# Split-precision Gram stage of a cross-attention kernel: one mixed product summed by whole rows, and a ring of ten high-high blocks

## The reference, cut to what matters

```
g     = g_w @ x_2 + g_b          # 256 x 1024
theta = theta_w @ x + theta_b    # 256 x 1024
phi   = phi_w @ x_2 + phi_b      # 256 x 1024
W     = theta.T @ phi / 1024     # 1024 x 1024
y     = (W @ g.T).T              # 256 x 1024
out   = batchnorm(w_w @ y + w_b) + x   # 512 x 1024, float32
```

## Time and profile before

| | us |
|---|---|
| median of 3 runs | 845.85 |
| lowest, highest | 845.2, 846.4 |
| span of the profiled execution, first to last instruction | 845.1 |
| TensorE matmul busy | 816.8 (97%) |
| TensorE weight loads busy | 708.9 (84%) |
| VectorE busy | 493.7 (58%) |
| ScalarE busy | 268.7 (32%) |
| GpSimd busy | 511.0 (60%) |

### The profile page before, as it was taken

How to read it: one execution, slowest core, us unless ns; L and a number is a source line. 1 busy time by engine, 2 the same in 40 slices (tenths; PEclk the granted TensorE clock), 3 DMA queues, 4 the chain that set the end, 5 groups by cost and what they waited for, 6 DMA issues and landing times.

```text
span 845.1 us, 12602 instructions
## 1 busy us (share of the span) xinstructions
PE 816.8 (97%) x4397; PEld 708.9 (84%) x4397; DVE 493.7 (58%) x885; ACT 268.7 (32%) x442; POOL 511.0 (60%) x351
## 2 busy tenths in 40 slices
PE   4589999999999999999999999999999999999997
PEld 2478888989889898988989888898988889898886
DVE  3865475565657556565655656565655766556254
ACT  1532333342233334223323412333242233323121
POOL 0893865668376565847666585666748556673400
PEclk9798999999999999999999999999999999999999
DMA  9825534254442434543253554325345432630202
GB/s 207 206 92 100 196 68 137 99 116 182 99 175 71 130 120 99 199 99 149 86 138 124 99 199 98 125 96 132 145 99 199 83 119 100 145 150 0 101 1 99
DMA packets 53010, 103.10 MB, mean 122 GB/s; under 512 B 2410, under 2 KB 35844, under 8 KB 52996
## 3 DMA queue, kind: packets, MB, share of 16 engines
q1 hardware_dynamic: 52996, 102.91, 41.5%
HBM read 69.35 MB, written 33.55 MB: 122 GB/s over the span
## 4 chain that ended last, share of the span: by engine, by line
PE 92%; DVE 3%; DMA 2%; POOL 1%; issue 1%; SPq 1%; ACT 0%; DVEq 0%; POOLq 0%; ACTq 0%
PE gbank L502 49%; PE wbank L502 42%; DMA ctx_sb<-in_ctx_dram 2%; PE wbank L602 1%; DVE ctxT_lo L390 1%; POOL x_lo L262 1%; DVE ctxT L354 1%; DVE gram_hi L432 1%; PE wbank L534 0%; SPq L199 0%; SPq L190 0%; POOL ctxT_lo L246 0%; POOL ctx_sum L254 0%; ACT x_hi L279 0%; DVE junk L420 0%
## 5 line engine op out<-in xcount | busy, mean ns | idle before, releaser
L246 POOL TENSOR_TENSOR ctxT_lo<-ctxT,ctxT_hi 128x512 fp32r<-128x512 f32 x120 | 158.5, 1320 | 147.8 <-ACT ctxT_hi L279 147.0
L262 POOL TENSOR_TENSOR x_lo<-x_sb,x_hi 128x1024 fp32r<-128x1024 f32 x64 | 151.8, 2406 | 110.1 <-ACT x_hi L279 110.1
L502 PE MATMUL gbank<-ctxT_hi,ctxT_lo 128*128 128x512 f32 (+3 forms) x512 | 165.8, 324 | 0.0
L502 PE MATMUL gbank<-ctxT_lo,ctxT_hi 128*128 128x512 f32 (+3 forms) x512 | 165.5, 323 | 0.0
L502 PE MATMUL gbank<-ctxT_hi 128*128 128x512 f32 (+3 forms) x512 | 163.4, 319 | 0.0
L279 ACT ACTIVATE ctxT_hi<-ctxT 128x512 fp32r<-128x512 f32 x128 | 80.3, 633 | 260.9 <-PE gbank L502 205.7
L254 POOL TENSOR_TENSOR ctx_sum<-ctx_sum,ctxT 128x512 f32<-128x512 f32 x112 | 155.7, 1390 | 0.9 <-POOL ctx_sum L249 0.2
L492 DVE SCALAR_TENSOR_TENSOR x_sb<-wbank,const,x_sb 128x512 f32<-128x512 f32 x128 | 89.4, 746 | 77.7 <-PE wbank L502 77.7
L354 DVE STREAM_TRANSPOSE ctxT<-ctx_sb 128x512 f32<-128x512 f32 x128 | 83.5, 689 | 56.7 <-POOL ctx_sum L254 28.1
L502 PEld LDWEIGHTS gbank<-ctxT_hi 128*128 128x128 f32 x512 | 97.6, 191 | 7.0 <-issue 0.2
L502 PEld LDWEIGHTS gbank<-ctxT_lo,ctxT_hi 128*128 128x128 f32 x512 | 96.8, 189 | 6.8
(11 more groups left out here) (92 smaller groups left out, 1342.7 us busy)
## 6 DMA issues: line engine op xcount, KB each, us to landing
ctx_sb<-in_ctx_dram SPq DMA_DIRECT2D x64, 512.0 KB, 8.4
x_sb<-in_x_dram SPq DMA_DIRECT2D x16, 2048.0 KB, 7.9
out_dram<-x_sb SPq DMA_DIRECT2D x64, 512.0 KB, 2.6
x_sb<-in_L_xattn_w_w_dram SPq DMA_DIRECT2D x1, 512.0 KB, 3.8
x_sb<-in_L_xattn_g_w_dram SPq DMA_DIRECT2D x1, 512.0 KB, 5.2
phi_nat<-in_L_xattn_phi_w_dram SPq DMA_DIRECT2D x1, 512.0 KB, 13.7
stage<-in_L_xattn_theta_w_dram SPq DMA_DIRECT2D x1, 512.0 KB, 12.5
bp_row<-in_L_xattn_phi_b_dram SPq DMA_DIRECT2D x1, 128.0 KB, 11.6
```

The source lines that it names most:

```text
L246: nc.gpsimd.tensor_tensor(ctxT_lo[:, c, :], src, f(ctxT_hi[:, c, :]), ALU.subtract).then_inc(ctxT_lo_made, 1)
L262: nc.gpsimd.tensor_tensor(x_lo[:, k, :], x_sb[par][:, k, :], f(x_hi[:, k, :]), ALU.subtract).then_inc(x_lo_made, 1)
L502: return nc.tensor.matmul(dst, lhsT, rhs, start=start, stop=stop, skip_group_check=True)
```

## The change

The high-high product is summed first, for all eight chunks, in four matmuls per chunk. It is held as ten of the sixteen 128 x 128 blocks, three, three and four in the three `gbank` banks, chosen as a ring: row blocks 0, 1 and 2 of widths 3, 3 and 2, and for row block 3 the blocks (3, 0) and (3, 3), read by one matmul with a step.

Then M = high x low is summed by whole rows, row block by row block, eight matmuls of 512 columns each, in two alternating `wbank` banks. ScalarE copies each row of M to the new tile `mt`. The product low x high is the transpose of M. It is no longer multiplied out: ten matmuls of `mt` against an identity (`turned`) add transposed blocks of M to `gbank`, and VectorE adds M itself when it takes the bank to `stage` (`PLAIN`, four additions). ScalarE, no longer VectorE, makes `gram_hi`. `t_hi` and `t_lo` now lie in `mt`.

`seq` and `own` are gone: each use has a fixed bank, and each wait names the event. S now has bank `wbank[4]`, is made after the rows of M, and theta(1) uses that bank next. TensorE therefore waits for `s_taken` ahead of theta(1). On VectorE the S work is split: the four reductions to `s_col` stand after `low_lo`, the two to `p1_raw` and the `p1` that raises `s_taken` stand after the last `t_lo`. The context chunks are four, two and two, at the start, after theta(0) and after `p1`, where they were six and two. `gram_chunk` is raised only in the last row of M. TensorE also waits ahead of the first batch until VectorE has freed all ten set-up groups.

```diff
+    HELD = [(0, 0), (0, 1), (0, 2), (1, 1), (1, 2), (1, 3), (2, 2), (2, 3), (3, 0), (3, 3)]
+    UPPER = len(HELD) * P
+    BANK_SPAN = [(0, 3 * P), (3 * P, 6 * P), (6 * P, UPPER)]
+    LOWER = [(3, 2), (0, 3), (1, 0), (2, 1), (3, 1), (2, 0)]
+
+
+    TURNED_EARLY = [(0, 0, 0), (1, 1, 0), (2, 2, 0), (3, 1, 1), (4, 2, 1), (6, 2, 2), (8, 0, 3)]
+    TURNED_LATE = [(5, 3, 1), (7, 3, 2), (9, 3, 3)]
+    LAST_OF_BANK = (2, 5, 9)
+
+    PLAIN = [(0, 3, 0), (3, 6, 5), (6, 9, 10), (9, 10, 15)]
     T_BANK = [0, 1, 2, 0]
     Q_BANK = [1, 2]
-    T_ORDER = [3, 2, 1, 0]
-
+    T_ORDER = [2, 3, 1, 0]
...
-        t_hi = sb("t_hi", [P, KC, CI], F32R)
-        t_lo = sb("t_lo", [P, KC, CI], F32R)
+        mt = sb("mt", [P, KC, C], F32R)
...
+        m_flat = mt[:, :, :].rearrange("p a b -> p (a b)")
+        t_hi = mt[:, 0:2, :].rearrange("p a (b c) -> p (a b) c", b=2)
+        t_lo = mt[:, 2:4, :].rearrange("p a (b c) -> p (a b) c", b=2)
...
+
+        M_BANK = [wbank[0], wbank[3], wbank[0], wbank[3]]
+        S_BANK = wbank[4]
+        LOW_BANK = [wbank[0], wbank[3]]
+        TH_BANK = [[wbank[1], wbank[2]], [wbank[4], wbank[0]]]
+        OUT_BANK = [[wbank[1], wbank[2]], [wbank[3], gbank[0]], [wbank[4], wbank[0]], [wbank[1], wbank[2]]]
...
-                if nxt:
-                    for c in range(EARLY):
-                        act.wait_ge(gram_chunk, (CH - 1) * b + (c + 1))
+                def next_hi(c):
+                    if nxt:
+                        act.wait_ge(gram_chunk, CH * b + (c + 1))
                         ctx_hi(b + 1, c)
+
+                for i in range(KC):
+                    if i < KC - 1:
+                        act.wait_ge(m_done, (KC - 1) * b + (i + 1))
+                    else:
+                        next_hi(0)
+                        act.wait_ge(gram_chunk, CH * b + CH)
+                    hi(mt[:, i, :], M_BANK[i][:, :], m_made)
+                next_hi(1)
                 for i, (a, z) in enumerate(BANK_SPAN):
-                    act.wait_ge(gram_row, 3 * b + (i + 1))
-                    hi(stage[:, a:z], gbank[i][:, 0:z - a], gram_f32)
+                    act.wait_ge(gram_f32, 3 * b + (i + 1))
+                    hi(gram_hi[:, a:z], stage[:, a:z], gram_hi_made)
+                next_hi(2)
                 for g in range(2):
-                    act.wait_ge(work_done, seq(b, G_LOW + g + 1))
+                    act.wait_ge(low_done, 2 * b + (g + 1))
                     hi(low_hi[:, 3 * g:3 * g + 3, :],
...
+                next_hi(3)
                 theta(0)
-                if nxt:
-                    for c in range(EARLY, CH):
-                        ctx_hi(b + 1, c)
+                next_hi(4)
+                next_hi(5)
                 for r, m in enumerate(T_ORDER):
                     act.wait_ge(t_taken, KC * b + (r + 1))
...
                 if nxt:
                     dve.wait_ge(in_ctx, b * (16 * QT) + 32 * QT)
-                    for c in range(EARLY):
...
-                nc.vector.tensor_tensor(p1[:, :], p1_raw[:, :], nbp_col[:, :], ALU.add).then_inc(work_free, 1)
+                for i, (a, z, m) in enumerate(PLAIN):
+                    g = min(i, 2)
+                    if i < 3:
+                        dve.wait_ge(gram_row, 3 * b + (i + 1))
+                    at = a * P - BANK_SPAN[g][0]
+                    ins = nc.vector.tensor_tensor(stage[:, a * P:z * P], gbank[g][:, at:at + (z - a) * P],
+                                                  f(m_flat[:, m * P:(m + z - a) * P]), ALU.add)
+                    if i != 2:
+                        ins.then_inc(gram_f32, 1)
                 for i, (a, z) in enumerate(BANK_SPAN):
...
+                dve.wait_ge(s_done, b + 1)
+                for i in range(KC):
+                    nc.vector.tensor_tensor_reduce(junk[:, 0, i * P:(i + 1) * P], S_BANK[:, i * P:(i + 1) * P], ident[:, :], 1.0, 0.0,
+                                                   ALU.mult, ALU.add, s_col[:, i:i + 1]).then_inc(s_made, 1)
                 theta(0)
                 if nxt:
-                    for c in range(EARLY, CH):
-                        transpose_chunk(b + 1, c, True)
+                    transpose_chunk(b + 1, 4, True)
+                    transpose_chunk(b + 1, 5, True)
+                dve.wait_ge(s_made, 6 * b + KC)
...
                     if r > 0:
                         t_lo_part(r - 1)
                 t_lo_part(KC - 1)
+                for k in range(KI):
+                    nc.vector.tensor_tensor_reduce(junk[:, k, :], S_BANK[:, :], phi_nat[:, k, :], 1.0, 0.0,
+                                                   ALU.mult, ALU.add, p1_raw[:, k:k + 1]).then_inc(s_made, 1)
+                dve.wait_ge(s_made, 6 * b + 6)
+                nc.vector.tensor_tensor(p1[:, :], p1_raw[:, :], nbp_col[:, :], ALU.add).then_inc(s_taken, 1)
+                if nxt:
+                    transpose_chunk(b + 1, 6, True)
+                    transpose_chunk(b + 1, 7, True)
 
...
                 for k in range(KI):
...
             pe.wait_ge(zb_taken, 1)
+            pe.wait_ge(work_free, SETUP_GROUPS)
+            pe.wait_ge(ident_r_made, 1)
...
+                def hi_of(c, i):
+                    return ctxT_hi[:, c, i * P:(i + 1) * P]
+
+                pe.wait_ge(work_free, NO * b + (SETUP_GROUPS + 4 - NO))
...
+                    pe.wait_ge(ctxT_hi_made, CH * b + (c + 1))
+                    mm(gbank[0][:, 0:3 * P], hi_of(c, 0), ctxT_hi[:, c, 0:3 * P], c == 0, False)
+                    mm(gbank[1][:, 0:3 * P], hi_of(c, 1), ctxT_hi[:, c, P:4 * P], c == 0, False)
+                    mm(gbank[2][:, 0:2 * P], hi_of(c, 2), ctxT_hi[:, c, 2 * P:4 * P], c == 0, False)
+                    mm(gbank[2][:, 2 * P:4 * P], hi_of(c, 3),
+                       ctxT_hi[:, c, :].rearrange("p (k q) -> p k q", q=P)[:, 0::3, :], False, False)
+
+                for i in range(KC):
+                    if i < 2:
+                        pe.wait_ge(work_free, NO * b + (SETUP_GROUPS + (6, 3)[i] - NO))
+                    else:
+                        pe.wait_ge(m_made, KC * b + (i - 1))
+                    for c in range(CH):
+                        if i == 0:
+                            pe.wait_ge(ctxT_lo_made, CH * b + (c + 1))
+                        ins = mm(M_BANK[i][:, :], hi_of(c, i), ctxT_lo[:, c, :], c == 0, c == CH - 1)
+                        if i == KC - 1:
+                            ins.then_inc(gram_chunk, 1)
+                    if i < KC - 1:
+                        ins.then_inc(m_done, 1)
+
+                pe.wait_ge(work_free, NO * b + (SETUP_GROUPS + 5 - NO))
+                pe.wait_ge(sum_split, 2 * b + 2)
+                mm(S_BANK[:, :], ones_r[:, :], sum_hi[:, :], True, False)
+                mm(S_BANK[:, :], ones_r[:, :], sum_lo[:, :], False, True).then_inc(s_done, 1)
+
+                def turned(blocks):
+                    for place, j, i in blocks:
+                        ins = mm(gram_bank(place), mt[:, j, i * P:(i + 1) * P], ident_r[:, :], False,
+                                 place in LAST_OF_BANK)
+                        if place in LAST_OF_BANK:
                             ins.then_inc(gram_row, 1)
...
+                pe.wait_ge(m_made, KC * b + 3)
+                turned(TURNED_EARLY)
+                pe.wait_ge(m_made, KC * b + 4)
+                turned(TURNED_LATE)
...
+                        if k == 0 and m == 0:
+                            pe.wait_ge(work_free, NO * b + SETUP_GROUPS)
+                        if k == 0 and m == 1:
+                            pe.wait_ge(s_taken, b + 1)
+                            pe.wait_ge(low_lo_made, 2 * b + 1)
...
                 pe.wait_ge(gram_lo_made, 3 * b + 3)
+                pe.wait_ge(low_lo_made, 2 * b + 1)
                 t_block(0)
-                pe.wait_ge(work_free, seq(b, G_LOW + 1))
                 t_block(1)
+                pe.wait_ge(low_lo_made, 2 * b + 2)
                 t_block(2)
-                pe.wait_ge(work_free, seq(b, G_LOW + 2))
                 pe.wait_ge(t_taken, KC * b + 1)
                 t_block(3)
                 theta(1, (0, 1))
...
                 pe.wait_ge(q_lo_made, KI * b + 1)
+                pe.wait_ge(th_lo_made, NT * b + NH)
+                pe.wait_ge(low_lo_made, 2 * b + 2)
+                pe.wait_ge(t_taken, KC * b + 4)
...
                 for m in (2, 3):
+                    if m == 3:
+                        pe.wait_ge(work_free, NO * b + (SETUP_GROUPS + NH))
```

More of the change, by code:

```diff
@@ L40, in xattn_kernel @@
     RING = 4
-    EARLY = 6
     assert CH * 32 == QN and NH * HALF == N
[L45 to L50, removed]
+    HELD = [(0, 0), (0, 1), (0, 2), (1, 1), (1, 2), (1, 3), (2, 2), (2, 3), (3, 0), (3, 3)]
[6 more added lines that the diff above has]
+    PLAIN = [(0, 3, 0), (3, 6, 5), (6, 9, 10), (9, 10, 15)]
     T_BANK = [0, 1, 2, 0]
     Q_BANK = [1, 2]
-    T_ORDER = [3, 2, 1, 0]
+    T_ORDER = [2, 3, 1, 0]
     NW = 5
     SETUP_GROUPS = 10
[L58 to L62, removed]
+    NO = KC * NH
```

(36 more changed lines are left out.)

70 lines of the change are left out of this document (25 added, 45 removed).

## The result

The changed kernel takes 918.5 us (median of 4 runs, 918.0 to 919.25) against 846.1 before on the same chip: a ratio of 1.085, 95% interval 1.084 to 1.0865. It is slower, by 72 us. The forecast was 926 in 884 to 948.

The account below looks back on a forecast made before the run. TensorE was taken to bound the kernel, any stall paid in full. Middle batch: -2.2 Gram, +5.4 stall, +2.4 clock = +5.6 us; 14 of them +78.4, last +2.1, first +0.3, on 845.1: span 925.9, forecast 926, range 884 to 948.

Parts of the forecast that it names:

- Gram stage: TensorE's Gram work per batch: 13.5 us in place of 15.75, a saving of 2.2, ends 0 to 2.3.
- The stepped operand: Gram matmul read with a step: might cost up to twice, 1.0 us more per batch; taken as ordinary.
- Its waits, and the split: New Gram waits and VectorE's split of G before the T blocks: no stall, split priced at zero, ends 0 to 1.5 us.
- the rival of a second stall: Ahead of the T blocks, where the split has no slack: 1.5 us more per batch, 949 us; chance 0.10.
- The wait ahead of theta(1): TensorE waits for `s_taken`, raised by VectorE's late `p1`: a 5.4 us stall per batch, ends 3.1 to 6.5.
- half of a shift of VectorE's T work: Four `s_col` reductions ahead of `th_lo` delay VectorE's T work by 0 to 0.6 us; half went into the stall.
- The clock: Behind the theta(1) stall the clock falls to half in every batch: 2.4 us each, ends 0 to 3.4.
- The sum: Whole kernel: middle batch +5.6 us, 14 of them +78.4, last +2.1, first +0.3; total +80.8, span 925.9.
- From the span to the time: Whole run: the runs' median lies 0.75 us above the span, so 925.9 becomes about 926.5, stated as 926.
- The clock holds: Behind the theta(1) stall: stall paid, no clock fall; middle batch +3.2 us, total about 890; chance 0.10.
- VectorE is not held up: T blocks without GpSimd in VectorE's way: stall 3.1 us, clock loss 1.8, total about 883 us; chance 0.10.
- Faster: `s_taken` comes less than 2.2 us after the last T block; hidden wholly, about 805 us; chance 0.04.

Follow-up runs that it names:

- the filler kernel: The changed kernel with 20 matmuls of 512 columns ahead of TensorE's wait for `s_taken`, into a bank nobody reads before it is overwritten: 886.3 us, ratio 1.047.
- the late chunks: The changed kernel with context chunks 4 and 5 moved behind `p1`, together with 6 and 7, so GpSimd rests beside the T blocks: 880.2 us, ratio 1.040.
- the other bank: The changed kernel with theta(1) in `wbank[3]` in place of S's `wbank[4]`, the outputs swapping the two, no engine's order changed: 810.7 us, ratio 0.958.

## Why the prediction was right, point by point
- *Gram stage.* Forecast 13.5 us, measured 13.52. The stepped operand cost nothing extra, and the transposed blocks overlap: ten of them, 434.45 to 435.52, take 1.07 where 0.9 was taken.
- *Its waits, and the split.* No idle time ahead of the turned blocks or the T blocks. The three `gram_lo` took 3.82 us, forecast 4.1. VectorE was done with the last `low_lo` 19.4 us after the batch's start, and the T blocks begin at 19.75: that much, 0.4 us, kept the rival of a second stall away.
- *The wait ahead of theta(1).* Forecast 5.4 us, measured 4.99 from the last T block's slot to theta(1) (idle 4.85), in the last batch 2.90 idle against 3.1. I had added half of a shift of VectorE's T work by the four reductions. There is none: VectorE idles 0.22 us between them and `th_lo` (L473, at 442.44), so they fill time in which it had to wait, and it takes up the T results 444.99 - 441.75 = 3.24 us after the T blocks begin, as before (417.90 - 414.66).
- *The clock.* Forecast 2.4 us per batch, 2.3 measured (5.03 against 2.74), 2.1 by the filler kernel. As the Trainium skill says in "TensorE: Matmul & The Clock Gate", section "HAM oscillation — how this bites in real kernels", the fall came with each pass, 16 times. The mean clock, forecast near 0.9, was 0.934.
- *A term that was missing.* A middle batch was to become 5.6 us longer and, once settled, is 4.86 longer. The stall is 0.4 less than forecast, the clock 0.1 less, and the output is 0.27 shorter, 10.88 where it took 11.15 (431.32 to 442.47). Before, a weight load of TensorE waited in it for up to 0.5 us in each batch (6.6 us, 16 times), and the next matmuls came late by part of that, as this row of the timeline of the kernel before shows for one:
```profile
432.82 0.30 PEld L502 LDWEIGHTS wbank<-th_hi,q_hi 128*128 128x128 f32 x2 [0.40 <-DVE th_lo L447]
```
  The rotation of banks explains it: `own` for the fourth output half (`G_OUT` + 3 = 10) waits until the use five places earlier is freed, and place 5 is the first half of theta(1), whose `th_lo` ends at 432.8. The fixed banks give row 1 of the output `wbank[3]` and `gbank[0]`, which theta(1) does not hold: in the changed kernel its first weight load comes at 466.86, before that `th_lo` (from 466.42, 0.75 us) ends. I had checked only that the new waits are early, and put the old ones at nothing.
- *The sum.* First batch and start +0.8 (forecast +0.3), 14 middle batches +67.2 (+78.4), the last and its tail +3.1 (+2.1): +71.2 on the span, 845.1 to 916.3. The forecast was +80.8. The middle batches lie 11.2 us below it, 0.8 each, and the two ends 1.5 us above it.
- *From the span to the time.* I took 0.75 us for what lies around the span, from one span and the median of other runs. Where span and time are those of the same run they differ by 1.8 or 1.9 us, after (918.1 against 916.3) as before (846.7 against 844.8). So the span missed by 9.6 us and the time, 926 against 918.5, by 7.5: part of the error is hidden by this one, which is luck.
- *Rivals.* "The clock holds" (890) is what the filler makes, 886.3; "VectorE is not held up" (883) is what the late chunks make, 880.2. Both prices were near, and neither case came by itself; in the second the clock loss was forecast for every batch and came in 11 of 16. "Faster" (805) is what the other bank makes, 810.7.

## What to carry to other kernels
When a shared buffer changes hands, look for the last reader's place in its engine's list, not for the time its work takes: 1.5 us of reductions stopped TensorE for 5 us per batch, since they stood behind work that is late by nature. Price the clock behind a stall too, and expect it to be given back in part when the stall moves. When a rotation of buffers is replaced by fixed ones, list the old waits that go as well as the new ones that come.

## What the runs showed of the hardware beyond that
The clock couples the length of a loop pass to itself. Each batch of the changed kernel stalls, so its clock falls and rises once; the lengths close in on 54.61 us, the distance halving from batch to batch (0.31, 0.18, 0.09, 0.06, 0.02). Its rises are 54.61 us apart from the first, however the restarts move, so a restart that comes later saves half of its delay at half the clock; that is the factor. What sets the distance of the rises was not tested. Small edits in such a kernel measure wrong: 7.3 us of added work showed as 2.2.

GpSimd and VectorE slow each other unevenly: beside GpSimd a `t_lo` goes from 0.42 to 1.12 us, while GpSimd's operations go from 1.30 to 1.48 (`ctx_sum` at 446.46 in the changed kernel), and to 1.75 beside `q_lo` (`sum_hi` at 409.55 in the kernel with another bank).
